# A quantised 3x3 convolution on one core: four edits in its first image (summed weights, rounding of the high weights, order of the scaling, pooling of the third image)

## The chip, the core and the metric

The kernel runs on one core of a Trainium2 chip. The time is that of the device in microseconds, from start to end of one execution of the program. Runs of the same kernel agree within about 0.3%.

## What is computed

Input x has 32 images of 128 channels and 56 x 56 pixels. Each 8 x 8 block of a channel goes, by its mean, to a path of 8 bits ("high") or one of 4 bits ("low"); the other path sees a small constant there. Both paths are quantised, convolved 3 x 3 (128 to 128 channels) with quantised weights, scaled and added.

```python
pooled = x.reshape(B, C, H // 8, 8, W // 8, 8).mean(axis=(3, 5))
mask = pooled >= 0.05                       # per block, spread over its 8 x 8 pixels
x_high = where(mask, x, EPS);  x_low = where(mask, EPS, x)
# activations: clip(round(x / scale), 0, 2**bits - 1) * scale
# weights, per output channel: s = max|w| / n, clip(round(w / s), -n, n) * s, n = 2**(bits-1) - 1
y = conv(quant_act(x_high, 8), quant_weight(w_high, 8)) + conv(quant_act(x_low, 4), quant_weight(w_low, 4))
```

## The kernel before

The 128 channels lie on the partitions. The program keeps integer values in f16 and works image by image. An image's 28 pairs of output rows are cut into four bands of 8, 8, 4 and 8 pairs (`BAND`, L42). For each band a two-row scheme computes both rows of a pair at once: a shared product T from sums of neighbouring rows ("row sums", `rowsum`), and products A and B from the rows themselves with weight differences, 15 matmuls in all, of 448 columns (224 in band 2). In band 3 of all images but the first, a cheaper form is used (`FAST`, products M0 to M3, 12 matmuls), which needs six summed weight matrices more, half of (outer taps plus or minus the middle tap) (`fast_weights`, L593), and differences of image rows (`differences`, L668).

Low and high products go into the same PSUM banks: TensorE writes the low products (`low`), ScalarE scales them in place by the ratio of the two output scales (`low_scaled`, L487), TensorE adds the high products (`high`), ScalarE makes a shared tile from T with the bias (`shared_tile`, L501), VectorE adds it to A and B and writes output rows (`out_row`, L712). Two sets of four banks alternate by band, so bands 0 and 2, and 1 and 3, use the same banks: the A product of low band 3 waits for the first output row of band 1 (L367).

Work for the next images is laid between: VectorE sums 8 x 8 blocks (`pool_blocks`, L612) and compares (`choose`); ScalarE spreads the result to pixels (`masks`, L453) and rounds x to int16 (`quantise`, L435); VectorE clips (`clip`), multiplies by the mask into `plane` (`apply_mask`, L639), and adds neighbouring rows (`row_sums`, L653).

Each engine takes its instructions strictly in the order in which the program writes them, and waits on semaphores. That order is written by hand, separately for image 0, the setup included (L391 for TensorE, L470 to L537 for ScalarE, L728 to L770 for VectorE, L300 to L312 for GpSimd). Weights are loaded once, scaled and rounded by VectorE (`weights`, L576), turned by TensorE through PSUM (`turn_weights`, L318; groups of 8, 7 and 6 matrices, banks in `TURN_BANKS`, L207), and copied by ScalarE (`turned_weights`, L463). TensorE also multiplies the turned weights by ones (`sum_weights`) for a constant that becomes the bias: ScalarE scales the sums (`eps_sum`), GpSimd combines them (L308 to L312). GpSimd else writes only borders of the planes (`borders`, L285). x is loaded and y stored by SP's queue: the load of image n + 2 waits until image n is pooled and rounded (L234), stores wait for output rows.

Images are counted from 0 here; the third image is image 2. "High band 1" means the high products of band 1.

Of the kernel before, what the change touches and what calls it, by code (L numbers as in the profile page):

```python
# [19 lines left out]
def conv_program(nc, x, w_high, w_low, scales, y):  # L20
# [13 lines left out]
    P = 128  # L34
# [28 lines left out]
    with ExitStack() as ctx:  # L63
# [27 lines left out]
        half_taps = {k: sb(f"half_taps_{k}", [P, 3, C], F16) for k in "hl"}  # L91
# [33 lines left out]
        s_border = [sem(f"borders_ready{p}") for p in range(2)]  # L125
        s_w_sum = {k: sem(f"w_sum_ready_{k}") for k in "hl"}
# [80 lines left out]
        TURN_BANKS = {"l": (3, 7, 3), "h": (4, 5, 3)}  # L207
# [67 lines left out]
        def _(pool):  # L275
# [23 lines left out]

            link = setup_link(pool, "gpsimd")  # L300
            borders(0)
            for k in "lh":
                pool.wait_ge(s_w_inv[k], 1)
                nc.gpsimd.tensor_tensor(out_scale[k][:, :], w_scale[k][:, :], act_scale[k], ALU.mult
                                        ).then_inc(s_out_scales, 1)
            borders(1)
            pool.wait_ge(s_out_scales, 2)
            for k in "lh":  # L308
# [3 lines left out]
                                    ).then_inc(s_bias, 1)  # L312

        @block.tensor
        def _(pe):
# [79 lines left out]
            def body(i, p, _):  # L395
# [3 lines left out]
                for pair in range(BANDS // 2):  # L399
                    if first_image(n) and pair == 0:  # L400
# [8 lines left out]
                        low(n, p, 1)  # L409
                        high(n, p, 1)  # L410
# [5 lines left out]
                    if first_image(n):  # L416

                        k = "lh"[pair]
                        pe.wait_ge(s_wq[k], 5)
                        if k == "l":  # L420
                            pe.wait_ge(s_eps_sum["l"], 1)
                        else:
                            pe.wait_ge(s_wT["l"], 3)
                        turn_weights(k, 2)

# [8 lines left out]
        def _(act):  # L434
# [382 lines left out]
```

## Time and profile before

| | us |
|---|---|
| median of 3 runs (lowest, highest) | 664.49 (664.17, 666.38) |
| the profiled execution, its own time | 662.33 |
| its span in the trace | 660.5 |
| busy: PE, DVE, ACT, POOL | 635.5, 594.5, 483.7, 10.2 |
| PE's share of the chain that ended last | 95% |

The profiled execution is one more execution, beside the three runs; its trace covers 660.5 us of its 662.33. PE is TensorE, DVE VectorE, ACT ScalarE, POOL GpSimd. A row of an engine's view in order of time gives its start, its duration, the line, the instruction with what it writes and reads, how many such instructions are merged, and in brackets how long the engine sat idle before it and what ended that.

### The profile page before, as it was taken

The numbers are of one execution on the slowest core, as the hardware profiler recorded it, in microseconds if no ns is written. First come the engines' busy times: TensorE is split into PE (matmuls) and PEld (weight loads), VectorE is DVE, ScalarE is ACT, GpSimd is POOL, SyncE is SP. The second block draws the span as 40 slices with busy tenths as digits, with TensorE's granted clock in tenths as the row PEclk, the third lists the DMA queues.
The fourth block names the chain that finished last, engine by engine and source line by source line (L and its number), as shares of the span: only waits on it lengthen the run. The fifth ranks groups of instructions, "written<-read, shape, count | busy, mean of one in ns | idle before, by whom it ended". The sixth has DMA issues, their size and how long they took to land.

```text
span 660.5 us, 10672 instructions
## 1 busy us (share of the span) xinstructions
PE 635.5 (96%) x3714; PEld 355.9 (54%) x3714; DVE 594.5 (90%) x739; ACT 483.7 (73%) x491; POOL 10.2 (2%) x30
## 2 busy tenths in 40 slices
PE   3779999999999999999999999999999999999996
PEld 1345555555555555555555555555555555555554
DVE  7899999999999999999999999999999999999933
ACT  6768787777777778778777778777877877877442
POOL 3200000000000000000000000000000000000000
PEclk9989999999999999999999999999999999999999
DMA  6245445533435543334543344553343454331122
GB/s 266 97 154 195 162 174 195 194 134 128 182 140 194 194 158 124 163 146 188 194 186 127 132 177 157 194 194 148 122 175 139 194 194 170 124 150 68 72 97 98
DMA packets 14409, 104.07 MB, mean 158 GB/s; under 512 B 1728, under 2 KB 1728, under 8 KB 10432
## 3 DMA queue, kind: packets, MB, share of 16 engines
q1 hardware_dynamic: 14400, 103.95, 41.2%
q8 instruction: 6, 0.10, 0.1%
q14 instruction: 3, 0.02, 0.0%
HBM read 52.56 MB, written 51.38 MB: 157 GB/s over the span
## 4 chain that ended last, share of the span: by engine, by line
PE 95%; ACT 2%; DVE 1%; DMA 1%; issue 0%; DVEq 0%; SPq 0%
PE psum L336 95%; DMA wraw_l<-w_low 1%; ACT rounded_h L450 0%; ACT psum L485 0%; ACT wT_l L467 0%; DVE pooled L619 0%; DVE w_max_l L578 0%; ACT wT_h L467 0%; PE psum L322 0%; DVE ybuf L717 0%; DVEq L63 0%; DVE wq_l L601 0%; DVE wint_l L585 0%; DVE upper L701 0%; DVE wq_l L590 0%
## 5 line engine op out<-in xcount | busy, mean ns | idle before, releaser
L485 ACT ACTIVATE psum<-psum,ratio 128x1344 f32<-128x1344 f32 (+2 forms) x159 | 174.4, 1097 | 131.0 <-PE psum L336 128.3
L336 PE MATMUL psum<-plane_l,wT_l 128*128 128x448 f16 (+1 forms) x1164 | 211.7, 330 | 0.0
L336 PE MATMUL psum<-plane_h,wT_h 128*128 128x448 f16 (+1 forms) x1164 | 209.5, 328 | 0.0
L336 PEld LDWEIGHTS psum<-plane_l,wT_l 128*128 128x128 f16 x1164 | 112.9, 97 | 83.1 <-issue 2.4
L336 PEld LDWEIGHTS psum<-plane_h,wT_h 128*128 128x128 f16 x1164 | 112.0, 96 | 81.3
L717 DVE SCALAR_TENSOR_TENSOR ybuf<-psum,out_scale_h,shared 128x448 f32<-128x448 f32 (+1 forms) x194 | 114.3, 605 | 27.5 <-PE psum L336 20.1
L619 DVE TENSOR_REDUCE pooled<-xbuf 128x49 f32<-128x3136 f32 (+2 forms) x33 | 109.4, 3315 | 0.0
L506 ACT ACTIVATE shared<-psum,bias,out_scale_h 128x448 f32<-128x448 f32 (+1 forms) x128 | 86.2, 674 | 26.4 <-PE psum L336 23.5
L450 ACT ACTIVATE rounded_l<-xbuf,inv_act_l 128x1568 int16<-128x1568 f32 (+1 forms) x64 | 101.7, 1591 | 4.8 <-DMA xbuf<-x 4.8
L450 ACT ACTIVATE rounded_h<-xbuf,inv_act_h 128x1568 int16<-128x1568 f32 (+1 forms) x64 | 101.9, 1594 | 0.0
L336 PE MATMUL psum<-rowsum_l,wT_l 128*128 128x448 f16 (+1 forms) x384 | 86.9, 335 | 2.3 <-ACT wT_l L467 2.3
L336 PE MATMUL psum<-rowsum_h,wT_h 128*128 128x448 f16 (+1 forms) x384 | 85.7, 331 | 2.6 <-ACT psum L485 2.5
L646 DVE TENSOR_TENSOR plane_l<-clipped_l,mask_l 128x3136 f16<-128x3136 f16 (+2 forms) x33 | 57.3, 1737 | 0.3 <-ACT mask_l L459 0.2
L646 DVE TENSOR_TENSOR plane_h<-clipped_h,mask_h 128x3136 f16<-128x3136 f16 (+2 forms) x33 | 57.3, 1737 | 0.0
L336 PEld LDWEIGHTS psum<-rowsum_h,wT_h 128*128 128x128 f16 x384 | 36.6, 96 | 31.7 <-issue 3.3
L336 PEld LDWEIGHTS psum<-rowsum_l,wT_l 128*128 128x128 f16 x384 | 36.8, 96 | 31.2 <-issue 3.0
L701 DVE SCALAR_TENSOR_TENSOR upper<-psum,neg_out_scale,shared 128x448 f32<-128x448 f32 x31 | 21.2, 684 | 27.1 <-PE psum L336 27.1
L336 PE MATMUL psum<-outer_h,wT_h 128*128 128x448 f16 x186 | 42.0, 360 | 0.0
L336 PE MATMUL psum<-outer_l,wT_l 128*128 128x448 f16 x186 | 42.0, 360 | 0.0
L635 DVE TENSOR_SCALAR clipped_h<-rounded_h,q_eps_h 128x3136 f16<-128x3136 int16 (+2 forms) x33 | 33.2, 1005 | 1.4 <-ACT rounded_h L450 1.4
L635 DVE TENSOR_SCALAR clipped_l<-rounded_l,q_eps_l 128x3136 f16<-128x3136 int16 (+2 forms) x33 | 33.1, 1003 | 0.0
L665 DVE TENSOR_TENSOR rowsum_l<-plane_l 128x1624 f16<-128x1624 f16 (+2 forms) x33 | 32.1, 972 | 0.3
(78 smaller groups left out, 340.4 us busy)
## 6 DMA issues: line engine op xcount, KB each, us to landing
xbuf<-x SPq DMA_DIRECT2D x31, 1568.0 KB, 6.5
y<-ybuf SPq DMA_DIRECT2D x32, 896.0 KB, 3.6
y<-ybuf SPq DMA_DIRECT2D x32, 672.0 KB, 3.9
xbuf<-x SPq DMA_DIRECT2D x1, 896.0 KB, 7.9
xbuf<-x SPq DMA_DIRECT2D x1, 672.0 KB, 5.3
wraw_l<-w_low SPq DMA_DIRECT2D x1, 576.0 KB, 4.1
wraw_h<-w_high SPq DMA_DIRECT2D x1, 576.0 KB, 6.2
act_scales<-scales SPq DMA_DIRECT2D x1, 1.0 KB, 1.8
```

The source lines that it names most:

```text
L336: last = nc.tensor.matmul(out, wT[k][:, mat, :], moving(k, p, band, row, dx), start=(k == "l" and j == 0), stop=(j == len(parts) - 1), ski ...
L450: nc.scalar.activation(rounded[k][p][:, part], xbuf[p][:, part], ACT.Relu, scale=inv_act[k][:, 0:1]).then_inc(s_round[k], 1)
L485: return nc.scalar.activation(banks, banks, ACT.Identity, scale=ratio[:, 0:1])
L506: nc.scalar.activation(shared[band % 2][:, 0:columns(band)], psum[:, BANK[band % 2]["T"], 0:columns(band)], ACT.Identity, bias=bias[:, 0:1 ...
L619: nc.vector.tensor_reduce(pooled[:, a0 * BX:a1 * BX].rearrange("p (a b) -> p a b", b=BX), xbuf[p][:, elements(q)].rearrange("p (a y b x) - ...
L635: nc.vector.tensor_scalar(clipped[k][:, elements(q)], rounded[k][p][:, elements(q)], 2.0 ** BITS[k][0] - 1.0, q_eps[k][:, 0:1], ALU.min, A ...
L646: nc.vector.tensor_tensor(rows(plane[k][p], (a0 * POOL + 1) * PITCH + 2, PITCH, (a1 - a0) * POOL).rearrange("p (a y) w -> p a y w", y=POOL ...
L665: nc.vector.tensor_tensor(rowsum[k][p][:, t0 * PITCH:t1 * PITCH].rearrange("p (t w) -> p t w", w=PITCH), source(1), source(2), ALU.add).th ...
L701: nc.vector.scalar_tensor_tensor(to[:, 0:columns(band)], tile(band, "M2"), scale[:, 0:1], shared[band % 2][:, 0:columns(band)], ALU.mult, ...
L717: nc.vector.scalar_tensor_tensor(y_rows(p, band, e), by_rows(tile(band, "AB"[e])), out_scale["h"][:, 0:1], by_rows(shared[band % 2][:, 0:c ...
```

## The change

Four edits, all in the setup and in image 0:

1. The summed weights (`fast_weights`) are made by GpSimd in place of VectorE, by four instructions for each path: outer taps added, plus and minus the middle tap, and one halving of 768 columns. Those of the low path stand before the borders of image 1's planes, those of the high path behind the bias. TensorE turns both sets before high band 1 of image 0, the high set through bank 7, and ScalarE copies them behind the masks of image 1.
2. The multiply and rounding of the high weights (`wint`) is a ScalarE activation; VectorE goes on with the clip and mask of the high plane meanwhile.
3. ScalarE scales low band 0 of image 0 ahead of the copies of the high weights, not behind. `low_ratio` is ahead of the first high row sums.
4. VectorE's order in image 0: mask and row sums of image 1 come before the output rows of bands 1 and 2, and the pooling of image 2 goes from ahead of these to the end. ScalarE's roundings of image 2 alternate with scalings and shared tiles.

```diff
-        half_taps = {k: sb(f"half_taps_{k}", [P, 3, C], F16) for k in "hl"}
+        tap_sums = {k: sb(f"tap_sums_{k}", [P, 6, C], F16) for k in "hl"}
...
-        TURN_BANKS = {"l": (3, 7, 3), "h": (4, 5, 3)}
+        TURN_BANKS = {"l": (3, 7, 3), "h": (4, 5, 7)}
...
+            def fast_weights(k):
+                pool.wait_ge(s_wq[k], 1)
+                nc.gpsimd.tensor_tensor(outer_taps[k][:, :, :], wq[k][:, 0:3, :], wq[k][:, 6:9, :], ALU.add
+                                        ).then_inc(s_taps[k], 1)
+                pool.wait_ge(s_taps[k], 1)
+                for at, op in ((0, ALU.add), (3, ALU.subtract)):
+                    nc.gpsimd.tensor_tensor(tap_sums[k][:, at:at + 3, :], outer_taps[k][:, :, :], wq[k][:, 3:6, :], op
+                                            ).then_inc(s_taps[k], 1)
+                pool.wait_ge(s_taps[k], 3)
+                nc.gpsimd.tensor_scalar(wq[k][:, GP:GP + 6, :], tap_sums[k][:, :, :], 0.5, 0.0, ALU.mult, ALU.add
+                                        ).then_inc(s_fast_wq[k], 1)
...
+            pool.wait_ge(s_out_scales, 2)
+            fast_weights("l")
             borders(1)
-            pool.wait_ge(s_out_scales, 2)
...
                                     ).then_inc(s_bias, 1)
+            fast_weights("h")
...
                         low(n, p, 1)
+                        pe.wait_ge(s_eps_sum["h"], 1)
+                        for k in "lh":
+                            pe.wait_ge(s_fast_wq[k], 1)
+                            turn_weights(k, 2)
                         high(n, p, 1)
...
             quantise("l", 0, 0, 1)
+            act.wait_ge(s_w_inv["h"], 1)
+            nc.scalar.activation(wint["h"][:, :, :], wraw["h"][:, :, :], ACT.Identity, scale=w_inv["h"][:, 0:1]
+                                 ).then_inc(s_wint["h"], 1)
             quantise("h", 0, 0, 1)
-            for m in range(2):
-                turned_weights("h", m)
...
                     low_scaled(n, 0)
+                    for m in range(2):
+                        turned_weights("h", m)
+                    masks(0, 0, 1)
...
-                    masks(0, 0, 1)
+                    quantise("l", 0, 1, 0)
                     shared_tile(n, 0)
-                    quantise("l", 0, 1, 0)
                     quantise("l", 0, 1, 1)
...
-                    turned_weights("l", 2)
                     masks(1, 1)
-                    for q in range(2):
-                        quantise("l", 1, 0, q)
+                    for k in "lh":
+                        turned_weights(k, 2)
+                    quantise("l", 1, 0, 0)
                     low_scaled(n, 2)
+                    quantise("l", 1, 0, 1)
                     low_scaled(n, 3)
                     shared_tile(n, 2)
+                    quantise("h", 1, 0, 0)
                     shared_tile(n, 3)
-                    for q in range(2):
-                        quantise("h", 1, 0, q)
-                    turned_weights("h", 2)
+                    quantise("h", 1, 0, 1)
...
-            weights("h")
+            weight_scale("h")
             clip("h", 0, 0, 0)
             apply_mask("h", 0, 0, 0)
+            weights("h")
+            low_ratio()
             row_sums("h", 0, 0, 0)
-            low_ratio()
...
                     clip("h", m, mp)
+                    apply_mask("l", m, mp)
+                    row_sums("l", m, mp)
                     out_rows(n, p, 1)
+                    apply_mask("h", m, mp)
+                    row_sums("h", m, mp)
                     for k in "lh":
-                        fast_weights(k)
+                        differences(k, m, mp, 3)
+                    out_rows(n, p, 2)
+                    out_rows(n, p, 3)
                     pool_blocks(1, 0)
                     choose(2)
...
```

`weight_scale` is the first part of the old `weights` (maximum, scale, inverse).

VectorE in image 0, behind the high clip of image 1, before; `ybuf` 128x8x56 are the output rows of band 1, `pooled` 128x49 is image 2's pooling:

```order
L717 SCALAR_TENSOR_TENSOR ybuf<-psum,out_scale_h,shared 128x8x56 [waits high_product,shared_ready]
L717 SCALAR_TENSOR_TENSOR ybuf<-psum,out_scale_h,shared 128x8x56 [waits high_product]
L595 TENSOR_TENSOR outer_taps_l<-wq_l 128x384 [waits wq_ready_l]
L597 TENSOR_SCALAR half_taps_l<-wq_l 128x384
L601 SCALAR_TENSOR_TENSOR wq_l<-outer_taps_l,half_taps_l 128x384 [waits tap_sums_ready_l]
L601 SCALAR_TENSOR_TENSOR wq_l<-outer_taps_l,half_taps_l 128x384
L595 TENSOR_TENSOR outer_taps_h<-wq_h 128x384 [waits wq_ready_h]
L597 TENSOR_SCALAR half_taps_h<-wq_h 128x384
L601 SCALAR_TENSOR_TENSOR wq_h<-outer_taps_h,half_taps_h 128x384 [waits tap_sums_ready_h]
L601 SCALAR_TENSOR_TENSOR wq_h<-outer_taps_h,half_taps_h 128x384
L619 TENSOR_REDUCE pooled<-xbuf 128x49 [waits x_loaded0]
L630 TENSOR_SCALAR chosen<-pooled 128x49 [waits mask_ready_l,mask_ready_h,x_pooled]
```

The same place now, from that clip up to the output rows of band 2 (128x4x56):

```order
L643 TENSOR_SCALAR clipped_h<-rounded_h,q_eps_h 128x3136 [waits rounded_ready_h]
L654 TENSOR_TENSOR plane_l<-clipped_l,mask_l 128x56x56 [waits mask_ready_l,clipped_ready_l]
L673 TENSOR_TENSOR rowsum_l<-plane_l 128x1624 [waits plane_ready_l,borders_ready1]
L725 SCALAR_TENSOR_TENSOR ybuf<-psum,out_scale_h,shared 128x8x56 [waits high_product,shared_ready]
L725 SCALAR_TENSOR_TENSOR ybuf<-psum,out_scale_h,shared 128x8x56 [waits high_product]
L654 TENSOR_TENSOR plane_h<-clipped_h,mask_h 128x56x56 [waits mask_ready_h,clipped_ready_h]
L673 TENSOR_TENSOR rowsum_h<-plane_h 128x1624 [waits plane_ready_h,borders_ready1]
L684 TENSOR_TENSOR outer_l<-plane_l 128x930 [waits plane_ready_l,borders_ready1]
L689 TENSOR_TENSOR inner_l<-plane_l 128x480
L684 TENSOR_TENSOR outer_h<-plane_h 128x930 [waits plane_ready_h,borders_ready1]
L689 TENSOR_TENSOR inner_h<-plane_h 128x480
L725 SCALAR_TENSOR_TENSOR ybuf<-psum,out_scale_h,shared 128x4x56 [waits high_product,shared_ready]
```

The eight instructions of the summed weights are gone; the low mask and row sums of image 1 (`plane_l`, `rowsum_l`) stand ahead of band 1's output rows, and the pooling does not follow here any more. It stands behind the output rows of band 3:

```order
L725 SCALAR_TENSOR_TENSOR ybuf<-psum,out_scale_h,shared 128x8x56 [waits high_product,shared_ready]
L725 SCALAR_TENSOR_TENSOR ybuf<-psum,out_scale_h,shared 128x8x56 [waits high_product]
L627 TENSOR_REDUCE pooled<-xbuf 128x49 [waits x_loaded0]
L638 TENSOR_SCALAR chosen<-pooled 128x49 [waits mask_ready_l,mask_ready_h,x_pooled]
L643 TENSOR_SCALAR clipped_l<-rounded_l,q_eps_l 128x3136 [waits rounded_ready_l]
```

What now follows the pooling is the threshold (`chosen`) and image 2's first clip, which before came twelve instructions further behind.

TensorE between low band 1 and low band 2 of image 0, before (L322 turns weights, `rowsum_h` begins high band 1, 128x224 is band 2):

```order
L336 MATMUL psum<-rowsum_l,wT_l 128x448 [waits rowsum_ready_l]
L336 MATMUL psum<-rowsum_l,wT_l 128x448 x2
L336 MATMUL psum<-plane_l,wT_l 128x448 x12
L336 MATMUL psum<-rowsum_h,wT_h 128x448 [waits low_scaled,rowsum_ready_h]
L336 MATMUL psum<-rowsum_h,wT_h 128x448 x2
L336 MATMUL psum<-plane_h,wT_h 128x448 x12
L322 MATMUL psum<-ident,wq_l 128x128 [waits eps_sum_ready_l,wq_ready_l]
L322 MATMUL psum<-ident,wq_l 128x128 x5
L336 MATMUL psum<-rowsum_l,wT_l 128x224 [waits shared_ready,rowsum_ready_l]
```

And now (L338 turns weights):

```order
L352 MATMUL psum<-rowsum_l,wT_l 128x448 x2
L352 MATMUL psum<-plane_l,wT_l 128x448 x12
L338 MATMUL psum<-ident,wq_l 128x128 [waits fast_wq_ready_l,eps_sum_ready_h]
L338 MATMUL psum<-ident,wq_l 128x128 x5
L338 MATMUL psum<-ident,wq_h 128x128 [waits fast_wq_ready_h]
L338 MATMUL psum<-ident,wq_h 128x128 x5
L352 MATMUL psum<-rowsum_h,wT_h 128x448 [waits low_scaled,rowsum_ready_h]
L352 MATMUL psum<-rowsum_h,wT_h 128x448 x2
L352 MATMUL psum<-plane_h,wT_h 128x448 x12
L352 MATMUL psum<-rowsum_l,wT_l 128x224 [waits shared_ready,rowsum_ready_l]
```

The turning of the low set moved from behind high band 1 to ahead of it, that of the high set came up from the end of image 0 to the same place, and both wait for GpSimd (`fast_wq_ready`).

## Rows read from the trace of the kernel before

**Rows 1.** Busy time by stretch: PE, PEld, DVE, ACT, POOL, granted clock, DMA share, GB/s.
```profile
18.90:21.80 2.90, 0.61 (x19) 0.46 (x16) 2.87 (x4) 2.90 (x5) 0.39 (x2) 1.00 0.15 26
...
36.70:48.00 11.30, 11.26 (x71) 7.08 (x72) 10.37 (x12) 9.63 (x11) 0.00 (x0) 0.85 0.44 148
...
80.00:640.00 560.00, 560.00 (x3268) 313.85 (x3266) 516.60 (x626) 417.20 (x422) 0.00 (x0) 1.00 0.41 158
```
**Rows 2.** TensorE in order of time: start, us taken, line, instruction, idle before it.
```profile
14.31 3.75 PE L336 MATMUL psum<-plane_l,wT_l 128*128 128x448 f16 x12
...
20.42 0.38 PE L328 MATMUL psum<-ones,wT_h 128*128 128x1 f16 x9 [1.32 <-ACT wT_h L467]
21.77 0.74 PE L336 MATMUL psum<-rowsum_h,wT_h 128*128 128x448 f16 x3 [0.97 <-ACT psum L485]
...
24.74 0.74 PE L336 MATMUL psum<-rowsum_l,wT_l 128*128 128x448 f16 x3
...
29.41 0.74 PE L336 MATMUL psum<-rowsum_h,wT_h 128*128 128x448 f16 x3 [1.54 <-ACT psum L485]
...
36.69 0.51 PE L322 MATMUL psum<-ident,wq_l 128*128 128x128 f16 x6 [4.16 <-DVE wq_l L601]
...
54.04 0.74 PE L336 MATMUL psum<-rowsum_h,wT_h 128*128 128x448 f16 x3
```
**Rows 3.** VectorE in order of time, 14 to 52 us.
```profile
14.48 0.85 DVE L585 TENSOR_SCALAR wint_h<-wraw_h,w_inv_h 128x1152 int16<-128x1152 f32 x1
...
17.04 0.86 DVE L646 TENSOR_TENSOR plane_h<-clipped_h,mask_h 128x1344 f16<-128x1344 f16 x1
...
32.92 1.04 DVE L635 TENSOR_SCALAR clipped_h<-rounded_h,q_eps_h 128x3136 f16<-128x3136 int16 x1 [1.35 <-ACT rounded_h L450]
33.87 1.27 DVE L717 SCALAR_TENSOR_TENSOR ybuf<-psum,out_scale_h,shared 128x448 f32<-128x448 f32 x2
35.05 0.35 DVE L595 TENSOR_TENSOR outer_taps_l<-wq_l 128x384 f16<-128x384 f16 x1
...
38.05 3.41 DVE L619 TENSOR_REDUCE pooled<-xbuf 128x49 f32<-128x3136 f32 x1
...
41.60 1.79 DVE L646 TENSOR_TENSOR plane_l<-clipped_l,mask_l 128x3136 f16<-128x3136 f16 x1
43.49 1.00 DVE L665 TENSOR_TENSOR rowsum_l<-plane_l 128x1624 f16<-128x1624 f16 x1
...
49.87 0.63 DVE L676 TENSOR_TENSOR outer_l<-plane_l 128x930 f16<-128x930 f16 x1
...
51.61 1.03 DVE L635 TENSOR_SCALAR clipped_l<-rounded_l,q_eps_l 128x3136 f16<-128x3136 int16 x1
```
**Rows 4.** ScalarE in order of time, 7 to 53 us.
```profile
7.04 1.42 ACT L450 ACTIVATE rounded_l<-xbuf,inv_act_l 128x1344 int16<-128x1344 f32 x1 [4.80 <-DMA xbuf<-x]
...
18.55 1.82 ACT L467 COPY wT_h<-psum 128x1024 f16<-128x1024 f16 x2 [2.04 <-PE psum L322]
20.25 1.38 ACT L485 ACTIVATE psum<-psum,ratio 128x1344 f32<-128x1344 f32 x1
...
49.87 0.62 ACT L459 ACTIVATE mask_l<-chosen,one 128x392 f16<-128x392 f16 x1
...
50.81 1.59 ACT L450 ACTIVATE rounded_l<-xbuf,inv_act_l 128x1568 int16<-128x1568 f32 x1
52.30 1.34 ACT L485 ACTIVATE psum<-psum,ratio 128x1344 f32<-128x1344 f32 x1
```
**Rows 5.** GpSimd in order of time, some rows from short windows.
```profile
1.28 0.29 POOL L281 TENSOR_SCALAR_AFFINE_SELECT ident<-ident 128x128 f16<-128x128 f16 x1 [0.24 <-POOL ident L279]
...
4.12 0.31 POOL L294 TENSOR_SCALAR plane_l<-zero,neg_q_eps_l 128x60 f16<-128x60 f16 x1 [2.54 <-DVE neg_q_eps_h L570]
...
17.12 0.96 POOL L294 TENSOR_SCALAR plane_h<-zero,neg_q_eps_h 128x60 f16<-128x60 f16 x1
...
22.58 0.98 POOL L311 TENSOR_TENSOR bias<-bias_part_h,bias_part_l 128x1 f32<-128x1 f32 x1
```

More of the change, by code:

```diff
@@ L125, in conv_program @@
         s_border = [sem(f"borders_ready{p}") for p in range(2)]
+        s_wint = {k: sem(f"w_rounded_{k}") for k in "hl"}
+        s_fast_wq = {k: sem(f"fast_wq_ready_{k}") for k in "hl"}
         s_w_sum = {k: sem(f"w_sum_ready_{k}") for k in "hl"}
@@ L415, in body @@
                         high(n, p, 2 * pair + 1)
[L416 to L424, printed above, removed]
             over_images(pe, body)
@@ L574, in act_scales, with weight_scale @@
                         last.then_inc(s_act, 1)
-            def weights(k):
+            def weight_scale(k):
                 dve.wait_ge(s_w[k], 16)
@@ L582, in weights @@
                 nc.vector.reciprocal(w_inv[k][:, :], w_scale[k][:, :]).then_inc(s_w_inv[k], 1)
-                dve.wait_ge(s_w_inv[k], 1)
+            def weights(k):
+                if k == "l":
+                    dve.wait_ge(s_w_inv[k], 1)
+                    nc.vector.tensor_scalar(wint[k][:, :, :], wraw[k][:, :, :], w_inv[k][:, 0:1], None, ALU.mult
+                                            ).then_inc(s_wint[k], 1)
                 top = 2.0 ** (BITS[k][1] - 1) - 1.0
-                link(nc.vector.tensor_scalar(wint[k][:, :, :], wraw[k][:, :, :], w_inv[k][:, 0:1], None, ALU.mult))
+                dve.wait_ge(s_wint[k], 1)
                 nc.vector.tensor_scalar(wq[k][:, 0:TAPS, :], wint[k][:, :, :], top, -top,
@@ L591, in weights @@
                                             ALU.subtract).then_inc(s_wq[k], 1)
-            def fast_weights(k):
-                dve.wait_ge(s_wq[k], 1)
-                nc.vector.tensor_tensor(outer_taps[k][:, :, :], wq[k][:, 0:3, :], wq[k][:, 6:9, :], ALU.add
-                                        ).then_inc(s_taps[k], 1)
-                nc.vector.tensor_scalar(half_taps[k][:, :, :], wq[k][:, 3:6, :], 0.5, None, ALU.mult
-                                        ).then_inc(s_taps[k], 1)
-                dve.wait_ge(s_taps[k], 2)
-                for at, op in ((GP, ALU.add), (GM, ALU.subtract)):
-                    nc.vector.scalar_tensor_tensor(wq[k][:, at:at + 3, :], outer_taps[k][:, :, :], 0.5,
-                                                   half_taps[k][:, :, :], ALU.mult, op).then_inc(s_wq[k], 1)
             def low_ratio():
@@ L728, in _ @@
             act_scales()
+            weight_scale("l")
             weights("l")
@@ L756, in body @@
                     clip("h", m, mp)
+                    apply_mask("l", m, mp)
+                    row_sums("l", m, mp)
                     out_rows(n, p, 1)
+                    apply_mask("h", m, mp)
+                    row_sums("h", m, mp)
                     for k in "lh":
-                        fast_weights(k)
+                        differences(k, m, mp, 3)
+                    out_rows(n, p, 2)
+                    out_rows(n, p, 3)
                     pool_blocks(1, 0)
                     choose(2)
-                    apply_mask("l", m, mp)
-                    row_sums("l", m, mp)
-                    out_rows(n, p, 2)
-                    apply_mask("h", m, mp)
-                    row_sums("h", m, mp)
-                    out_rows(n, p, 3)
-                    for k in "lh":
-                        differences(k, m, mp, 3)
                     return
```

## The prediction

> **What bounds the kernel now.** I read three views: busy time by stretch, then each engine's instructions in order of time over the first 62 us, then GpSimd's few instructions one by one. By stretch [rows 1], TensorE is busy for all 560.00 us between 80 and 640 us, VectorE for 516.60 of them. An edit in the first image can only move the moment at which that dense stretch begins. So the question is what TensorE loses before it.
>
> TensorE's rows [rows 2] show where. It waits 1.32 and 0.97 us before high band 0 (the second time for ScalarE's scaling), 1.54 us before high band 1, then 4.16 us for VectorE's summed weights. Behind that last wait the granted clock of 36.7 to 48.0 is 0.85 of full [rows 1]: part of it ran at 1.2 GHz, not 2.4. At 0.15 of 11.3 us that cost 1.7 us. The reader is to see that the large loss is one place, and that VectorE has no free time behind it.
>
> I count from two moments of TensorE: X, when high band 1 of image 0 starts (29.41), and Y, when high band 0 of image 1 starts (54.04) [rows 2]. Behind Y all is dense, so the change of Y is the change of the span. Of the 24.63 us between, a 448-column tile set takes 2.97 (24.74 less 21.77) [rows 2] and a 224-column one half of it; the five of the first kind and two of the second between X and Y make 17.8 us. The rest, 6.8 us, is waits, the clock and the twelve transposes.
>
> **The change, part by part.**
>
> *Weights of the high path.* The rounding multiply leaves VectorE, which gains 0.85 us [rows 3], and goes to ScalarE. ScalarE did 1,344 columns in 1.42 us [rows 4], so 1,152 take about 1.2 us. It sits where ScalarE waited 2.04 us for TensorE [rows 4]; cost nothing. If ScalarE had no such wait, low scaling would start 1.2 us later.
>
> *Scaling ahead of the weight copies.* The low product of band 0 ends at 18.06 (14.31 + 3.75) [rows 2]. The scaling starts there and takes 1.38, then the copies 1.82 [rows 4]: 18.06 + 1.38 + 1.82 = 21.26. The nine summing matmuls (0.38) [rows 2] follow, and high band 0 starts at 21.65, not 21.77. The distance from it to X was 7.64 us (29.41 less 21.77) and is not touched, so X = 29.3: 0.1 us gained, if the scale ratio is ready at 18.06. VectorE would have it at about 17.5: the clip of the high part starts in place of the rounding at 14.48, and what stood between the rounding and the mask moves with it.
>
> *Summed weights.* VectorE loses the eight instructions between 35.05 and 38.05 [rows 3]: 3.00 us. Both sets of transposes now stand before X, in a wait, and leave the stretch between X and Y. Twelve take about half a microsecond (six took 0.51 at 36.69) [rows 2], so set h must be there by 28.8 for X to hold.
>
> *VectorE behind X.* High clip started 3.51 us behind X (32.92 less 29.41) [rows 2, 3] and still does, since ScalarE's work ahead of it is the same. Now come the low mask and row sums of image 1 before the output rows of band 1: clip 0.95 (to 33.87), mask 1.89 (43.49 less 41.60), row sums 1.00, half of the pair of output rows 0.64 (1.27) [rows 3], so the first output row is done at X + 8.0. TensorE had finished high band 1, low band 2 and three matmuls of low band 3 at X + 5.05 and needs that bank. **A new wait of 2.95 us** takes the place of the 4.16. From X + 8.0: twelve matmuls (2.4), high band 2 (1.49), high band 3 (2.97): image 0's last product is at X + 14.85.
>
> *Pooling of the third image.* VectorE does the high mask, row sums and differences (1.89 + 1.00 + 1.74, the last from 49.87 to 51.61), then output rows of bands 2 and 3 [rows 3]. Those wait for TensorE until X + 14.85, and the pooling, now behind them, starts at X + 15.6. It takes 3.6 with its threshold (38.05 to the next instruction at 41.60 is 3.55) [rows 3]: X + 19.2. ScalarE's masks (0.94), one rounding (1.49) and the scaling of low band 0 of image 1 (1.34) stand behind it [rows 4] in that order, each start taken from the next: X + 23.0, and Y = X + 23.3 with the handovers. Before, the pooling was done at 41.6 and the masks waited only for ScalarE (49.87). TensorE arrives at X + 20.8: **a second new wait, 2.5 us.** On SP the load of image 4 waits for this pooling, and the store of image 0's second half is queued behind that load. Both move to about 49 us; image 4 is rounded only while image 2 is multiplied, some 13 us behind Y, and the output buffer is written again then: nothing waits for either.
>
> So Y = 29.3 + 23.3 = 52.6, and the change is worth **1.4 us** at best: 3.0 and 0.85 us come off VectorE, but the wait is split, not removed.
>
> *What GpSimd makes of it.* The trace has no GpSimd instruction of 384 columns. From below: 60 columns took 0.31 us [rows 5], so an instruction takes at least that. From above: the select of 128 columns took 0.29 [rows 5]; three times that is 0.87 for 384 and six times 1.74 for 768. I take 0.7 and 0.9, well under the upper ends, since part of 0.29 is there at any length: 3.0 us a set, alone. But GpSimd does not work beside VectorE [rows 3, 5]: the 60-column instruction at 17.12 took 0.96 and ended at 18.08, just behind the two-input multiply that ran from 17.04 to 17.90. Set l starts at 14.7, behind the high scale, and with a wait at each instruction is done by about 20. Eight borders follow, at 0.31 to 0.96 each: 2.5 us alone, 5 to 7 if all were slowed; I take 2.5 to 5, since VectorE's pooling of one input falls there: 22.5 to 25. The bias takes some 1.6 (its last instruction alone 0.98 [rows 5]) after the later of those and of ScalarE's two sums (about 22.5), set h 3.2 to 4 after that: 27.3 to 30.6. So everything on GpSimd is queued behind its wait for the high scale, and the bias gates ScalarE's shared tile.
>
> How much VectorE waits for GpSimd, no row shows: the multiply beside a border instruction took 0.86 for 1,344 columns, and one with GpSimd at rest 1.79 for 3,136 (at 41.60) [rows 3], no slower by length than a fixed part explains. The bounds are nothing and the whole length of four instructions, 3.0 us and handovers of 0.3, for the ratio and all behind it. The nearest row speaks for little, but it is short. I take a third, 1.1 us, of which 0.6 is slack, and 0.4 more for a late set h: **X = 30.2, Y = 53.5, a gain of 0.5 us**. The profiled execution would go from 662.33 (span 660.5 and 1.8 around it) to 661.8. The runs' median was 664.49, 2.2 above that execution, so I give 664.0.
>
> The Trainium skill (SBUF — State Buffer, "SBUF: two separate sides") says that the port VectorE and GpSimd share is an exclusive lock, so that whoever comes second waits for the whole instruction. The row at 17.12 agrees for GpSimd as the second. No row here shows VectorE as the second; by that rule it would wait out each of the four, and the time would be that of the first rival. The skill's GPSIMD Engine Reference ("Elementwise — side-by-side cycle accounting") has a two-input add of 2,048 columns at 4,497 ns, by which 384 would be an estimated 0.84 us; the sum would then have set h 0.4 us later.
>
> **The rivals.** A difference of 0.3% is 2.0 us, about what a measurement here can tell.
>
> *Slower: VectorE is held by GpSimd.* If each instruction of set l holds the next of VectorE's, the ratio is ready at 20.8, the scaling starts 2.7 us late, high band 0 at 24.35, X = 32.0, Y = 55.3: 1.3 us slower. TensorE would then do only fifteen transposes and nine short matmuls between 18.1 and 24, longer than the 4.16 us behind which the clock fell before; another 1.7 us. Price: +3.0, 667.5. It decides when X, with half the clock's price in it, passes 32.7 (30.7 is where the gain ends, and 2.0 more the bound). For it: the blocking at 17.12. Against: VectorE's multiply beside GpSimd's border was hardly longer.
>
> *Faster: the clock.* One stretch at 1.2 GHz cost 1.7 us in the profiled execution, and the ordinary runs are 2.2 us longer than it; they may lose the clock for longer. The two new waits, 2.95 and 2.5 us, are shorter than 4.16 and near the idle time between 18.9 and 21.8 (TensorE busy 0.61 of 2.90 us, clock 1.00) [rows 1], after which full speed held. With no loss at all, and X on time, the gain over such runs is 1.4 + 1.7 = 3.1: 661.4. Against: nothing shows that those runs lost clock there.
>
> *The wait only moves.* If GpSimd's instructions run at the upper rows (4.35 us a set, and a wait at each), set h is ready at 30.5 to 31.5, X is 31 to 32 and the change does not do what it says: +0.3 to +1.3, 664.8 to 665.8. It lies inside the forecast's bound.
>
> **How the numbers follow.** The forecast has 0.35 and the wait that only moves 0.15; both are within 2.0 us of 664.49, 0.5 together. The slower rival has 0.3: its mechanism is half seen, its size needs the clock as well. The faster one 0.2. The forecast's own range is 663.0 (X on time) to 665.0. Over all, with about one tenth left out on each side, it is 661.0 (the faster rival and what one run differs from the next) to 667.5.
>
> **What would show it.** Right: no VectorE row of summed weights; TensorE waiting 2 to 3.5 us for output rows in low band 3, again for scaling before high band 0 of image 1; ScalarE's masks for image 2 starting on the threshold; image 1's high band 0 at 52.5 to 54.5. The slower rival: VectorE's masks and clips behind 15 us stretched or late, the ratio behind 19.5, granted clock below full around 20 to 28 us. The faster: granted clock 1.00 from 30 to 56 us. Wrong altogether if TensorE waits anywhere behind image 1, or if Y stands more than 3 us from 53.5.

## The result, and the profile after

| | before | after |
|---|---|---|
| median of 14 runs each, same chip (lowest, highest), us | 662.41 (661.71, 666.38) | 666.96 (665.09, 668.1) |
| ratio after / before, 95% interval | | 1.0056 [1.0041, 1.007] |
| the profiled execution, its own time, us | 662.33 | 667.96 |
| its span in the trace, us; mean granted clock of TensorE | 660.5; 0.996 | 666.1; 0.988 |

The change makes the kernel slower by 0.41 to 0.70%, which is 2.7 to 4.6 us. "No difference" was forecast, with a chance of 0.3 for slower. The time is inside the range of 661.0 to 667.5; the sign is that of the slower rival. The two profiled executions lie 5.6 us apart in span, more than the interval, so part of what follows is larger in them than in most runs. The runs of the kernel before scatter over 5 us (0.7%, more than the 0.3% given at the start) and their median differs from job to job (662.41, 663.99, 662.29), so every ratio below is taken within its own job.

First the busy time by stretch of the kernel after (columns as in [rows 1]):

```profile
20.00:26.90 6.90, 4.27 (x25) 1.86 (x22) 6.66 (x9) 5.77 (x10) 5.39 (x12) 0.62 0.59 196
...
40.50:44.00 3.50, 2.80 (x10) 1.25 (x11) 3.40 (x5) 2.18 (x2) 0.00 (x0) 0.73 0.87 366
...
57.50:61.20 3.70, 3.14 (x12) 1.41 (x13) 2.81 (x3) 3.70 (x4) 0.00 (x0) 0.73 0.97 303
80.00:640.00 560.00, 560.00 (x3269) 314.08 (x3268) 519.38 (x629) 421.06 (x426) 0.00 (x0) 1.00 0.41 157
```

From 80 to 640 us TensorE is as full as before, so the loss lies ahead of 80 us again. There are now three stretches below full clock (0.62, 0.73, 0.73) where before there was one. TensorE in order of time shows what stands ahead of each; these rows answer to [rows 2]:

```profile
14.30 4.38 PE L352 MATMUL psum<-plane_l,wT_l 128*128 128x448 f16 x12
...
22.74 0.40 PE L344 MATMUL psum<-ones,wT_h 128*128 128x1 f16 x9 [2.63 <-ACT wT_h L477]
23.00 1.28 PE L352 MATMUL psum<-rowsum_h,wT_h 128*128 128x448 f16 x3
24.08 4.60 PE L352 MATMUL psum<-plane_h,wT_h 128*128 128x448 f16 x12
28.52 0.74 PE L352 MATMUL psum<-rowsum_l,wT_l 128*128 128x448 f16 x3
...
33.19 0.74 PE L352 MATMUL psum<-rowsum_h,wT_h 128*128 128x448 f16 x3 [0.87 <-ACT psum L496]
...
41.20 3.91 PE L352 MATMUL psum<-plane_l,wT_l 128*128 128x448 f16 x12 [2.81 <-DVE ybuf L725]
...
46.71 0.74 PE L352 MATMUL psum<-rowsum_h,wT_h 128*128 128x448 f16 x3
...
58.06 0.74 PE L352 MATMUL psum<-rowsum_h,wT_h 128*128 128x448 f16 x3 [2.29 <-ACT psum L496]
58.64 4.15 PE L352 MATMUL psum<-plane_h,wT_h 128*128 128x448 f16 x12
62.63 0.74 PE L352 MATMUL psum<-rowsum_h,wT_h 128*128 128x448 f16 x3
```

X is 33.19 and Y 58.06. The 4.16 us wait for the summed weights is gone, and waits of 2.81 and 2.29 us stand in its place. Ahead of high band 0, where the kernel before idled 1.32 and 0.97 us, there is now one wait of 2.63. Behind each of the three the twelve 448-column matmuls take 4.60, 3.91 and 4.15 us, not 2.55. High band 0 takes 5.52 us (28.52 less 23.00) against 2.97 before: 2.55 lost. Low band 3 and high band 2 behind the second wait lose 1.4 (5.51 us from 41.20 to 46.71; the experiment with all waits filled, below, needs 4.09, from 38.20 to 42.29). High band 0 of image 1 loses 1.6 (4.57 against 2.97). Together that is 5.55 us, against the 1.7 that the one stretch cost before.

VectorE, which answers to [rows 3], and GpSimd, which answers to [rows 5]:

```profile
15.99 0.89 DVE L605 TENSOR_SCALAR wq_h<-wint_h 128x1152 f16<-128x1152 int16 x1 [0.20 <-ACT wint_h L490]
16.91 1.94 DVE L609 TENSOR_TENSOR wq_h<-wq_h 128x384 f16<-128x384 f16 x2
...
18.95 0.60 DVE L615 TENSOR_TENSOR ratio<-out_scale_l,inv_high 128x1 f32<-128x1 f32 x1
```

```profile
15.03 1.54 POOL L304 TENSOR_TENSOR outer_taps_l<-wq_l 128x384 f16<-128x384 f16 x1
16.64 1.99 POOL L308 TENSOR_TENSOR tap_sums_l<-outer_taps_l,wq_l 128x384 f16<-128x384 f16 x2
18.72 0.83 POOL L311 TENSOR_SCALAR wq_l<-tap_sums_l 128x768 f16<-128x768 f16 x1
...
26.19 0.91 POOL L304 TENSOR_TENSOR outer_taps_h<-wq_h 128x384 f16<-128x384 f16 x1
27.17 2.07 POOL L308 TENSOR_TENSOR tap_sums_h<-outer_taps_h,wq_h 128x384 f16<-128x384 f16 x2
29.33 0.83 POOL L311 TENSOR_SCALAR wq_h<-tap_sums_h 128x768 f16<-128x768 f16 x1
```

The three VectorE rows lie beside set l, the summed weights of the low path (set h is that of the high path). In the kernel before, the rows of the same tiles, beside border instructions, took less, and the ratio took 0.16:

```profile
15.36 0.46 DVE L586 TENSOR_SCALAR wq_h<-wint_h 128x1152 f16<-128x1152 int16 x1
15.86 0.66 DVE L590 TENSOR_TENSOR wq_h<-wq_h 128x384 f16<-128x384 f16 x2
```

They now take 0.89, 1.94 and 0.60. The ratio ends at 19.55. ScalarE, which answers to [rows 4], passes that on:

```profile
14.71 1.25 ACT L490 ACTIVATE wint_h<-wraw_h,w_inv_h 128x1152 int16<-128x1152 f32 x1
...
19.59 1.35 ACT L496 ACTIVATE psum<-psum,ratio 128x1344 f32<-128x1344 f32 x1 [1.96 <-DVE ratio L615]
...
54.15 0.62 ACT L469 ACTIVATE mask_l<-chosen,one 128x392 f16<-128x392 f16 x1 [3.60 <-DVE chosen L638]
```

Scaling starts on the ratio and the weight copies stand behind the scaling, so TensorE's sums of the high weights wait until 22.74. In the last row image 2's masks wait for the threshold behind the moved pooling.

Two causes are in the rows, and they are mixed: late work (GpSimd beside VectorE, then VectorE's new order) and what the waits do to the clock. The theory taken into the experiments was that both count and the clock counts more; the rival, that the lateness of the ratio alone carries everything.

### The profile page after: what moved, and what is told of

Read it like the earlier page. It is cut to its first block, busy times and chain, and to the rows that moved or that the text cites. A ratio compares the mean times of both kernels' runs of the same rounds, so it can differ in the third digit from the quotient of the medians.

```text
span 666.1 us, 10671 instructions
## 1 busy us (share of the span) xinstructions
PE 640.4 (96%) x3714; PEld 356.9 (54%) x3714; DVE 593.7 (89%) x730; ACT 485.1 (73%) x492; POOL 17.7 (3%) x38
## 4 chain that ended last, share of the span: by engine, by line
PE 93%; DVE 2%; ACT 2%; issue 1%; DMA 1%; DVEq 0%; SPq 0%
PE psum L352 93%; DVE pooled L627 1%; DMA wraw_l<-w_low 1%; ACT psum L496 1%; ACT rounded_l L460 0%; ACT rounded_h L460 0%; DVE wq_h L609 0%; DVE plane_l L654 0%; ACT wT_h L477 0%; ACT wT_l L477 0%; DVE w_max_l L591 0%; ACT wint_h L490 0%; DVEq L63 0%; DVE wq_h L605 0%; DVE wint_l L601 0%
## 5 line engine op out<-in xcount | busy, mean ns | idle before, releaser
L352 PE MATMUL psum<-plane_h,wT_h 128*128 128x448 f16 (+1 forms) x1164 | 213.2, 331 | 0.0
L673 DVE TENSOR_TENSOR rowsum_h<-plane_h 128x1624 f16<-128x1624 f16 (+2 forms) x33 | 32.7, 990 | 0.2
```

The costliest lines, as they stand in the source:

```text
L352: last = nc.tensor.matmul(out, wT[k][:, mat, :], moving(k, p, band, row, dx), start=(k == "l" and j == 0), stop=(j == len(parts) - 1), ski ...
L673: nc.vector.tensor_tensor(rowsum[k][p][:, t0 * PITCH:t1 * PITCH].rearrange("p (t w) -> p t w", w=PITCH), source(1), source(2), ALU.add).th ...
```

## Experiments

Eight kernels, each timed against the kernel before; times are us. The extra matmuls of four of them go to a bank whose content is overwritten before it is read.

**1. Set l behind the ratio** (the kernel after, one wait added on GpSimd):

```diff
             pool.wait_ge(s_out_scales, 2)
+            pool.wait_ge(s_ratio, 1)
             fast_weights("l")
```

> The changed kernel, but GpSimd starts the low summed weights only when VectorE has made the scale ratio, so that they run beside the one-input pooling. If GpSimd's instructions held VectorE's (port theory): VectorE's high weights take 0.46 us, not 0.89, the two differences about 0.65, not 1.94, the ratio is there by 17.7 us, not 19.55, high band 0 starts near 21.7, not 23.0; and with a shorter wait the clock may stay up, which gives the 5.5 us of high band 0 back to 3.0. Time 663 to 665.5 where the changed kernel has 667.0. If VectorE is slow there for another reason (ScalarE's rounding of the same weights, the new order): ratio still behind 19 us and 667. If the low set then comes too late, TensorE waits for it ahead of high band 1.

Measured: 666.29, ratio 1.004 [1.0025, 1.0055]. VectorE's rows in this kernel, then TensorE's:

```profile
15.62 0.46 DVE L606 TENSOR_SCALAR wq_h<-wint_h 128x1152 f16<-128x1152 int16 x1 [0.19 <-ACT wint_h L491]
16.12 0.63 DVE L610 TENSOR_TENSOR wq_h<-wq_h 128x384 f16<-128x384 f16 x2
...
16.86 0.16 DVE L616 TENSOR_TENSOR ratio<-out_scale_l,inv_high 128x1 f32<-128x1 f32 x1
...
17.42 2.02 DVE L628 TENSOR_REDUCE pooled<-xbuf 128x28 f32<-128x1792 f32 x1
```

```profile
20.89 0.38 PE L345 MATMUL psum<-ones,wT_h 128*128 128x1 f16 x9 [2.21 <-ACT wT_h L478]
...
21.71 2.55 PE L353 MATMUL psum<-plane_h,wT_h 128*128 128x448 f16 x12
...
31.93 0.82 PE L339 MATMUL psum<-ident,wq_h 128*128 128x128 f16 x6 [4.37 <-POOL wq_h L311]
...
33.67 4.06 PE L353 MATMUL psum<-plane_h,wT_h 128*128 128x448 f16 x12
```

The same instructions in the same order, without set l beside them, take 0.46, 0.63 and 0.16: GpSimd did hold VectorE, by 0.43 + 1.31 + 0.44 = 2.2 us. High band 0 starts 1.9 us earlier, about half of it because low band 0 begins and ends earlier in this execution (3.70 us for its twelve matmuls, not 4.38), and runs at full clock. But the gain is not kept. The borders now run beside VectorE's clips and masks (three of 60 columns take 3.52 us from 21.42, against 1.28 in the kernel after), the bias and set h are queued behind them, set h ends at 31.87, and TensorE waits 4.37 us for it, with half the clock behind. The wait had only moved. Of the two later waits of the kernel after, that for output rows shrinks to 0.85 us, and that for scaling ahead of image 1 stays at 2.29.

**2. The first wait filled** (the kernel after):

```diff
                         sum_weights("l")
+                        for _ in range(7):
+                            nc.tensor.matmul(psum[:, 6, 0:N_MAX], wT["l"][:, 0, :], moving("l", p, 0, None, 0),
+                                             start=True, stop=True, skip_group_check=True)
                         sum_weights("h")
```

> The changed kernel with seven more 448-column matmuls into an unused bank, put into TensorE's first wait (ahead of the sums of the high weights); nothing else is moved. If the loss behind that wait is the clock: granted clock at its full level from 23 us, high band 0 takes 3.0 us and not 5.5, high band 1 starts at 30.7 and not 33.2, time 664.5. If the idle time is not what drops the clock, or high band 0 is slow for another reason: 5.5 us as before and 667; if the matmuls last beyond the wait, up to 0.5 us worse.

Measured: 665.28, ratio 1.002 [1.0005, 1.0036]. TensorE:

```profile
22.70 0.74 PE L352 MATMUL psum<-rowsum_h,wT_h 128*128 128x448 f16 x3
23.28 2.55 PE L352 MATMUL psum<-plane_h,wT_h 128*128 128x448 f16 x12
...
29.93 0.51 PE L338 MATMUL psum<-ident,wq_h 128*128 128x128 f16 x6 [0.80 <-POOL wq_h L311]
...
38.35 4.15 PE L352 MATMUL psum<-plane_l,wT_l 128*128 128x448 f16 x12 [2.80 <-DVE ybuf L728]
```

High band 0 starts when it did, 22.70 for 23.00, and takes 2.55 for the twelve, not 4.60: what slowed it was TensorE's idling ahead of it, and nothing in its data. X comes to 30.34. The second and third wait stay, at 2.80 and 2.29, with the clock lost behind both.

**3. VectorE's old order** (the kernel after, with the pooling and the output rows of image 0 where the kernel before had them, plus a wait that keeps the blocks' results apart):

```diff
                     clip("h", m, mp)
+                    out_rows(n, p, 1)
+                    dve.wait_ge(s_chosen, prepared(1))
+                    pool_blocks(1, 0)
+                    choose(2)
                     apply_mask("l", m, mp)
                     row_sums("l", m, mp)
-                    out_rows(n, p, 1)
+                    out_rows(n, p, 2)
                     apply_mask("h", m, mp)
                     row_sums("h", m, mp)
+                    out_rows(n, p, 3)
                     for k in "lh":
                         differences(k, m, mp, 3)
-                    out_rows(n, p, 2)
-                    out_rows(n, p, 3)
-                    pool_blocks(1, 0)
-                    choose(2)
```

> The changed kernel with VectorE's order of image 0 as in the kernel before (output rows of band 1, pooling of image 2, then mask and row sums of image 1), the three other edits kept. If the two waits of TensorE (2.8 us for output rows in low band 3, 2.3 us for the scaling of image 1's low band 0) come from the order alone: both gone or under 1 us, image 1's high band 0 about 18 to 19.5 us behind image 0's high band 1, not 24.9, and with them the two later half-clock stretches: 658 to 661. If VectorE's sum of work is the bound whatever its order: the waits come back elsewhere (for row sums or output rows of image 1), 665 to 667.

Measured: 660.38, ratio 0.9948 [0.9932, 0.9964]: faster than the kernel before. TensorE:

```profile
22.95 0.38 PE L344 MATMUL psum<-ones,wT_h 128*128 128x1 f16 x9 [2.62 <-ACT wT_h L477]
...
23.77 4.14 PE L352 MATMUL psum<-plane_h,wT_h 128*128 128x448 f16 x12
...
32.41 0.74 PE L352 MATMUL psum<-rowsum_h,wT_h 128*128 128x448 f16 x3 [0.87 <-ACT psum L496]
...
43.29 0.74 PE L352 MATMUL psum<-rowsum_h,wT_h 128*128 128x448 f16 x3 [1.10 <-ACT psum L496]
...
52.20 0.74 PE L352 MATMUL psum<-rowsum_h,wT_h 128*128 128x448 f16 x3
```

The first wait is as in the kernel after, with a smaller loss of clock behind it (4.14 us for the twelve, not 4.60). The second and third wait are gone (1.10 us is the longest that is left), and Y stands 19.8 us behind X, not 24.9. VectorE's new order alone turns a gain into a loss: 0.9948 against 1.0056. The edit takes back the whole order. By the rows, the second wait, for output rows, comes of the low mask and row sums put ahead of band 1's output rows, and the third, behind the threshold, of the moved pooling; the two were not taken back one by one.

**4. Both**: the wait of experiment 1 in the kernel of experiment 3.

> Both changes together (low summed weights behind the ratio, old order of VectorE). If port, clock and order are three separate terms that add: the gains of the two single runs add, 655 to 658, below the kernel before (662.4). If they overlap (the same stall seen twice): no better than the better of the two.

Measured: 660.95, ratio 0.9957 [0.9939, 0.9974]. The gains do not add: as in experiment 1, high band 0 runs early and at full clock, and TensorE then waits for set h (the twelve matmuls behind take 4.40):

```profile
32.04 0.82 PE L339 MATMUL psum<-ident,wq_h 128*128 128x128 f16 x6 [4.03 <-POOL wq_h L311]
```

**5. The borders early** (experiment 4, with image 1's borders ahead of GpSimd's wait for the high scale, where it idled):

```diff
                                         ).then_inc(s_out_scales, 1)
+                if k == "l":
+                    borders(1)
...
             fast_weights("l")
-            borders(1)
```

> The changed kernel with the old order of VectorE (as in the third run) and on GpSimd the borders of image 1's planes ahead of the high scale, where GpSimd was idle for 6.6 us, and the low set behind the ratio. If the two first repairs failed to add only because the borders, held up by VectorE, made the high set late: no wait for GpSimd ahead of high band 1, high band 0 near 21.6 at full clock, high band 1 near 29.5 and the time 1 to 1.3% under the kernel before (655 to 657 where that has 663.5). If GpSimd cannot make set h in time beside VectorE at all: a wait of 2 us or more ahead of high band 1 and no better than 0.5% under.

Measured: 657.44, ratio 0.9907 [0.9882, 0.9931]. TensorE no longer waits for GpSimd:

```profile
22.39 0.38 PE L346 MATMUL psum<-ones,wT_h 128*128 128x1 f16 x9 [2.13 <-ACT wT_h L479]
...
23.72 3.61 PE L354 MATMUL psum<-plane_h,wT_h 128*128 128x448 f16 x12
...
31.84 0.74 PE L354 MATMUL psum<-rowsum_h,wT_h 128*128 128x448 f16 x3 [0.87 <-ACT psum L498]
```

High band 0 came at 22.64 and X at 31.84, not at the 21.6 and 29.5 expected. The profiled execution took 659.91, 2.5 above the median of its runs, and it lost clock in high band 0 (3.61 us for the twelve). Its mean clock was 0.997 and that of the other five 0.997 to 1.000, but one of 657.31 had 0.997 too, so the clock is not all of the 2.5; no trace of another run exists.

**6. The wait of the kernel before filled** (17 matmuls of 512 columns in the 4.16 us):

```diff
+                        if k == "l":
+                            pe.wait_ge(s_eps_sum["l"], 1)
+                            busy(3, 17)
```

> The kernel before with 17 more matmuls (512 columns, into an unused bank) inside TensorE's wait of 4.16 us for VectorE's summed weights. If the half-clock stretch behind that wait costs what its row says: granted clock full from 37 us on and 1.5 to 2 us (0.25 to 0.3%) faster than the kernel before. If the clock has another cause: no change, or a little slower if the matmuls outlast the wait.

Measured: 661.74, ratio 0.9987 [0.997, 1.0004]: no difference that can be told. The clock held (mean 0.999), but of the 1.7 us 1.11 came back as a wait for ScalarE's scaling that the slower matmuls had covered:

```profile
42.42 0.45 PE L342 MATMUL psum<-rowsum_h,wT_h 128*128 128x224 f16 x3 [1.11 <-ACT psum L494]
...
53.16 0.74 PE L342 MATMUL psum<-rowsum_h,wT_h 128*128 128x448 f16 x3
```

Y is 0.88 earlier, 0.36 of it because this execution's early rows are all earlier. So a lost clock costs what it stretches only as far as no later wait takes that time up.

**7. All three waits of the kernel after filled** (6, 10 and 8 such matmuls):

```diff
+                    if first_image(n) and band == 3:
+                        pe.wait_ge(s_wT["l"], 3)
+                        busy(3, 10)
...
                         sum_weights("l")
+                        busy(6, 6)
                         sum_weights("h")
...
+                        if isinstance(n, int) and n == 1 and pair == 0:
+                            busy(3, 8)
```

> The changed kernel, order kept, with more matmuls in each of its three waits of 2.3 to 2.8 us. If the clock makes up the slowdown and the waits themselves are no longer than before: no half-clock stretch before the last 5 us, the span 5 to 5.5 us under the changed kernel's 666.1, so 660.5 to 661.5, level with or just under the kernel before. If port and order alone make it: 664 or more in spite of the full clock.

Measured: 662.19, ratio 0.998 [0.9964, 0.9996]; twelve runs from 661.91 to 662.52. TensorE:

```profile
30.18 0.74 PE L358 MATMUL psum<-rowsum_h,wT_h 128*128 128x448 f16 x3
...
38.20 2.56 PE L358 MATMUL psum<-plane_l,wT_l 128*128 128x448 f16 x12 [0.53 <-DVE ybuf L737]
...
42.29 0.74 PE L358 MATMUL psum<-rowsum_h,wT_h 128*128 128x448 f16 x3
...
53.65 0.74 PE L358 MATMUL psum<-rowsum_h,wT_h 128*128 128x448 f16 x3 [0.56 <-ACT psum L508]
```

The change's work and its lateness are in this kernel: VectorE is held as in the kernel after (the row below), the pooling is late, the output rows come at X + 8.0. Only TensorE idles less: of the three waits 1.31, 0.53 and 0.56 us are left.

```profile
18.52 0.61 DVE L627 TENSOR_TENSOR ratio<-out_scale_l,inv_high 128x1 f32<-128x1 f32 x1
```

The span is 660.1, 6.0 less than that of the kernel after. High band 0 starts 0.45 earlier in this execution (22.55); the 5.55 that are left are the sum of the three losses above, and the whole loss is gone. This separates the theories: had the late ratio carried the loss, it would have stayed.

**8. A version with both causes out** (experiment 5, and: output rows of band 3 ahead of the high mask on VectorE; on ScalarE scaling of bands 2 and 3 ahead of the masks of image 1 and the second roundings, the copies of the summed weights moved into image 1; six matmuls in the first wait):

```diff
+                        busy(6, 6)
...
+                    low_scaled(n, 2)
                     masks(1, 1)
-                    for k in "lh":
-                        turned_weights(k, 2)
                     quantise("l", 1, 0, 0)
-                    low_scaled(n, 2)
-                    quantise("l", 1, 0, 1)
                     low_scaled(n, 3)
                     shared_tile(n, 2)
-                    quantise("h", 1, 0, 0)
+                    quantise("l", 1, 0, 1)
                     shared_tile(n, 3)
+                    quantise("h", 1, 0, 0)
...
+                if isinstance(n, int) and n == 1:
+                    for k in "lh":
+                        turned_weights(k, 2)
...
+                    out_rows(n, p, 3)
                     apply_mask("h", m, mp)
                     row_sums("h", m, mp)
-                    out_rows(n, p, 3)
```

> As the borders-early kernel, and: both output rows of bands 2 and 3 ahead of the high mask of image 1 on VectorE; on ScalarE the scaling of low band 2 ahead of the masks of image 1, that of band 3 and its shared tile ahead of the second rounding, the last weight copies moved into image 1; six matmuls into TensorE's first wait. If what is left behind high band 1 is waits for scalings (0.4 and 1.1 us in the third run): image 1's high band 0 at 18.0 to 18.5 us behind image 0's high band 1 (19.8 in the third run) and 0.5 to 1.5 us under the borders-early kernel. If VectorE's work is the bound by now: no difference.

Measured: 657.19, ratio 0.9901 [0.9877, 0.9924]. It beats both kernels; experiment 5 does so as well, and the two can't be told apart. TensorE:

```profile
48.55 0.74 PE L360 MATMUL psum<-rowsum_h,wT_h 128*128 128x448 f16 x3
...
55.47 1.38 PE L360 MATMUL psum<-plane_l,wT_l 128*128 128x224 f16 x12 [0.53 <-DVE ybuf L735]
...
59.03 0.76 PE L360 MATMUL psum<-outer_l,wT_l 128*128 128x448 f16 x3 [0.42 <-DVE ybuf L735]
```

Y is 18.5 us behind X (30.07), so little is left between them beside 17.8 us of products. VectorE's output rows are late next: 0.95 us of waits in image 1 that no other kernel here had.

## Why the prediction was wrong

**The working order came out as written.** The rounding on ScalarE took 1.25 us (1.2 forecast) and lies inside its old idle time. The first output row was to be done at X + 8.0: TensorE went on at 41.20, X + 8.01. The second wait was put at 2.95 and measured 2.81; the third at 2.5, measured 2.29, behind the chain of pooling, threshold, masks, rounding and scaling that was named. Y was to follow X by 23.3; it does so by 24.87, of which 1.4 is clock. Without the clock (experiment 7) X is 30.18 and Y 53.65; 30.2 and 53.5 were forecast. That X agrees so closely is partly luck: high band 0 came 0.9 late there (22.55), where the sum had 0.5, and the late set h, put at 0.4 on top, cost nothing from there to X (7.63 us, against 7.64 in the kernel before, which waited for scaling instead). The later load of image 4 cost nothing, as was said: TensorE is busy for all 560.00 us from 80 us on.

**GpSimd's own time was sized a little short.** 0.7 and 0.9 us were taken for one instruction; it was 0.91 (and 2.07 for two) and 0.83, so a set takes 4.0 us and not 3.0. Set h ended at 30.16, inside the 27.3 to 30.6. Where X was not late for other reasons, TensorE waited 0.8 us for it (experiments 2 and 7); 0.4 was in the sum.

**The step "I take a third, 1.1 us, of which 0.6 is slack" was mis-sized.** The ratio was forecast for about 17.5 and ended at 19.55, about 2.0 later; experiment 1 gives 2.2 for the stretching alone. The upper bound had been 3.3. The row that was called nearest, a multiply beside a border instruction, was that of a VectorE instruction that had begun first. The Trainium skill (SBUF — State Buffer, "SBUF: two separate sides") says that of a GpSimd instruction and a VectorE instruction that is in a two-port mode or has two SBUF inputs, whichever starts first keeps the shared port for its whole instruction. The trace now agrees for VectorE as the second: the two-input subtractions begin at 16.91 inside GpSimd's 16.64 to 18.63 and take 1.94 us, not 0.63; the cast to `wq_h` begins at 15.99 inside GpSimd's 15.03 to 16.57, ends at 16.88, and takes 0.89 us, not 0.46. The upper bound did not come true either. VectorE held GpSimd too: its multiply of the plane had begun at 14.93, and GpSimd's first instruction behind it took 1.54 us, against 0.91 for the same form in set h. That this is why the bound was missed is argued, not shown. High band 0 started at 23.00, 1.35 later than the 21.65 of the sum. Not all of it is this step's: scaling started 0.9 us behind the end of low band 0, and most of the rest is low band 0 itself, which took 4.38 where [rows 2] have 3.75.

**The step that decided was the sum's: Y = X + 23.3 gives every new wait its own length and nothing for the clock behind it, and takes the 1.7 us of clock as saved.** Its ground is in the faster rival: the two new waits "are shorter than 4.16 and near the idle time between 18.9 and 21.8", "after which full speed held". Measured: 5.55 lost behind three waits of 2.63, 2.81 and 2.29 us. The stretch of 18.9 to 21.8 was the wrong row to stand on: its idle time lay in two pieces of 1.32 and 0.97 us with matmuls between, and the new waits are each one piece. There was also a third that the sum did not name: with the scaling ahead of the copies, those two pieces become one, about 2.1 us by the sum's own times (TensorE done at 18.74 + 0.37 as in the kernel before, the copies at 21.26), 2.21 in experiment 1 and 2.63 in the kernel after. From the sum's best case, 1.4 us gained: 1.35 late, 5.55 of clock (the 1.7 of before is already gone in the best case) gives 5.5 slower, against 5.6 in the spans. Y itself came at 58.06, 4.6 from the 53.5 of the forecast, which by the prediction's own last sign is wrong altogether; the other 1.6 us of the span lie behind Y, where the prediction took all to be dense.

**The slower rival had the mechanism and the order of events** (held ratio, late scaling, late high band 0, then the clock behind it), with a chance of 0.3, and its signs were met: the ratio behind 19.5, a granted clock of 0.62 from 20.0 to 26.9. It was wrong in its sizes: the ratio 1.25 us earlier than it said, the clock lost at three places and not at one. It also thought of the clock as a consequence of VectorE being held; experiment 2 cured the first place and left the second and third, experiment 1 the third, and these come from VectorE's new order. Taking that order back (experiment 3) was worth about 1% of the time, more than any other single edit to the kernel after.

**That the time lies in the range is partly luck.** The range was built on three runs of the kernel before with a median of 664.49; over 14 it is 662.41. The change cost 4.6 us, where the slower rival, the upper end of the range, had 3.0.

**Left open.** Whether the port or something else in the memory makes VectorE wait was not tried, for instance with GpSimd instructions of the same length that read nothing. The rounding on ScalarE and the scaling ahead of the copies were not taken out by themselves. Why the twelve matmuls of low band 0 take 3.52 to 4.69 us in different executions no row tells: the granted clock reads 1.00 there. The two causes within VectorE's new order (output rows, pooling) were not separated.

## What to carry to other kernels

Price a wait of TensorE as its length plus what the clock does behind it: here one wait of 2.3 to 2.8 us cost 1.4 to 2.6 us more, so a wait of 4.16 exchanged for such waits was no gain. A later wait can take up part of that price (1.1 of 1.7 us in experiment 6). Before work is moved to GpSimd, look at what VectorE does in those microseconds; the same four instructions left a reduction at its length and held a chain of short instructions by 2 us, and what is queued behind them on GpSimd is moved as well. To learn whether a loss is lateness or clock, fill the wait with matmuls whose result nobody reads: in experiments 2, 6 and 7 the lateness stayed and the clock did not fall behind the filled waits.

## What the runs showed that had not been expected

The clock fell behind single waits of 2.29 to 2.81 us in every profiled execution that had one, and behind one of 2.13 in part (experiment 5: 3.61 us for the twelve); behind 2.21 (experiments 1 and 4) it did not, nor behind the filled waits, of which 0.49 to 1.31 us were left idle. So the length of the wait alone does not decide.

The scatter of the runs goes with the clock. The mean granted clock of each run is on record for the two later jobs: of the kernel before, the 28 runs up to 662.65 us have 0.995 or 0.996, the 22 from 663.13 to 664.90 have 0.993, and the three from 666.06 to 666.53 have 0.989. A step of 0.003 to 0.004 over 660 us is 2.0 to 2.6 us, about the distance of these groups. So many runs of the kernel before lost more clock than the one that was profiled, which the faster rival had guessed; where, no trace shows. It is not the 4.16 us wait alone: with that wait filled (experiment 6), nine runs have 0.999 and take 661.30 to 662.14, and three have 0.996 and take 663.83 to 664.59. With all three waits of the kernel after filled (experiment 7) all runs have 0.998 or more and lie within 0.6 us.

VectorE's pooling was not stretched by GpSimd: 2.02 us beside set l in experiment 1, 2.01 in the kernel before. The short instructions behind it were: the threshold of 128x28 took 0.70 in place of 0.22 in the kernel after, and in the kernel after itself the ratio of 128x1 took 0.60 in place of 0.16.
